# Pad rows, weight halves and weight loads in another order around the seam between routing and experts

## The chip, the cores and the metric

The kernel is one program on one core of a Trainium2 chip. The metric is the device time of one execution in microseconds (us). Of the kernel before there are three timed runs; the profiled execution is a fourth.

## The reference, cut to what matters

The layer is attention with a window of 64, followed by a mixture of experts: 2048 rows of 256 values, 16 experts of which each row goes to 4, and one shared expert that takes every row.

```python
h = _layernorm(x) * (1 + ca) + sa
x = x + ga * attention(h, w_qkv, w_out)          # 16 heads of 16, window 64
h = _layernorm(x) * (1 + cb) + sb
probs = softmax(abs((h @ ru.T) * silu(h @ rg.T)))
_, idx = top_k(probs + extra_bias, 4)            # 4 of 16 experts for a row
w = 1 + probs * extra_scale                      # taken at idx
y = sum over e of (silu(h @ Wg[e].T) * (h @ Wu[e].T)) @ Wd[e].T * c[:, e]
z = (silu(h @ Sg.T) * (h @ Su.T)) @ Sd.T
x = x + gb * (y + z)
```

Everything is float32. A product is made of three passes: each operand is split in a high half (rounded) and a low half (what the rounding left), and high by high, low by high and high by low are added.

## The kernel before, in words

**Stages.** `project_qkv` and `attention_and_routing` stand in one block of instructions, `experts_and_output` in a second. Between the two every engine reaches the end of its own list, drains, and waits until all have (the records of this are on L1999). The seam lies at about 312 to 338 us of the span.

**The end of the first block.** GpSimd sends the routed rows of the last tile pairs to `xs_scr` in DRAM by indirect DMAs (`dispatch`, `send_rows`, L140; one of 128 rows each). The rows of an expert are padded up to a multiple of 128: `fill_up` (L182 to L184) writes one block of 128 pad rows behind each of the 16 experts, as soon as the counts are known (`tb`). SyncE writes the pads of experts 0 to 10, ScalarE those of 11 to 15. An issue is a load of the place from `pad_i` and a DMA of 144 KB.

**Weights.** `raw` holds the 16 experts' weights: experts 0 to 7 are loaded in the attention stage, 8 to 14 by ScalarE at 290 us (semaphore `w_rest`), 15 by GpSimd in the second block (`w_last`, L190 and L191), which loads the shared expert's weights too (`sgu_raw`, `sdn_raw`). High halves are made by ScalarE: `split_hi` (L174 for gate and up, L175 for down). Low halves of gate and up are made by VectorE (`gu_low`, L1795, 128x704), those of down by GpSimd (`dn_low`, L1688, 88x512).

**The expert steps.** 79 steps of 128 rows of one expert each. For step s SyncE loads the rows (`load_x`, L1584, to `x_st`, four in flight: the first four at once, each further one after its buffer was transposed and `picked`), TensorE transposes them (L1859), ScalarE makes the high half of the transposed rows (L1620) and VectorE the low half (`x_lo`, L1743). TensorE makes gate and up (`GU`, L105), ScalarE the silu (L1626), VectorE the product (`gating`, L1755); that is transposed (`HT`, L1869), split (L1633, L1748) and multiplied by down (`YP`, L105). VectorE scales the result (L1763) and GpSimd sends it to `ys_scr` (L1709). The order of each engine's list is the order in the code. TensorE's list begins: transpose the rows of step 0, those of step 1, `GU` of step 0, transpose those of step 2, `GU` of step 1, transpose those of step 3, and so on. Step s of the first 16 waits for `gu_lo` of s + 1, and from step 2 on for `dn_lo` of s - 1.

**What sets the places of the halves.** `HI_IN_TAIL` is 11: `split_hi` of experts 0 to 10 stands in the first block. `LO_AHEAD` is 5: `gu_low` of five experts stands ahead of step 0, and `LOW_STEPS` lists the steps that each make one more. `FIRST` is 8.

Of the kernel before, what the change touches and what calls it, by code (L numbers as in the profile page):

```python
# [19 lines left out]
NE, TOPK, FI = 16, 4, 176  # L20
# [21 lines left out]
W_EXP = W_GU + W_DN  # L42
HW = D + 2 * NE
IDS = D + NE
HI_IN_TAIL, HI_AHEAD, LO_AHEAD = 11, 13, 5
LOW_STEPS = (0, 1, 3, 4, 5, 7, 8, 9, 11, 12, 13)
PLACES = TOPK * S_LEN
LD = 3 * 16

# [621 lines left out]
def attention_and_routing(nc, A, T, ctx, own):  # L671
# [122 lines left out]
    def _(eng):  # L794
# [78 lines left out]
        keep_x1(LAST, 3)  # L873
        keep_h2(PAIRS - 1, 1)
        eng.wait_ge(tb, TB_PAD)
        fill_up(nc, eng, A, T, 0, 11)
        for t in range(4):
            eng.wait_ge(x1_st[t], 32 * (TILES // 4) + 32)
            if t < 2:
# [4 lines left out]
    def _(eng):  # L884
# [102 lines left out]
        router_exp(PAIRS - 1, 1)  # L987
        for e in range(4, FIRST):
            split_hi(eng, T, e)
        eng.wait_ge(tb, TB_PAD)  # L990
        fill_up(nc, eng, A, T, 11, NE)
        eng.wait_ge(T["w_rest"], 64)
        for e in range(FIRST, HI_IN_TAIL):
            split_hi(eng, T, e)

    @block.gpsimd
# [460 lines left out]
def experts_and_output(nc, A, T, out, ctx, own):  # L1457
# [226 lines left out]
    @block.gpsimd  # L1684
    def _(eng):
        def dn_low(e):
            eng.wait_ge(w_hi2, 2 * e + 2)
            eng.tensor_tensor(lo[0:FH, e, W_GU:W_EXP], raw[0:FH, e, W_GU:W_EXP],  # L1688
                              dn_hi[0:FH, e, :].bitcast(F32), ALU.subtract).then_inc(dn_lo, 1)

        for e in range(3):
            dn_low(e)
        load_raw(eng, A, T, NE - 1, NE, w_last)
        eng.dma_start(sgu_raw[:, :, :, :], A["sgu"]).then_inc(sgu_ld, 16)
        eng.dma_start(sdn_raw[:, :, :], A["sd"]).then_inc(sdn_ld, 16)
        for e in range(3, FIRST):
            dn_low(e)
        for p in range(2):
            eng.wait_ge(sent[p], 32)

        def step(s, r, i, first, last):
            q = r // 2 % 2
            if r % 2 == 0 and runs(s, 4):

                eng.wait_ge(sent[q], 32 * i + 32)
                plain(eng)
            eng.wait_ge(y_out, s + 1)
            plain(eng)
            eng.indirect_dma_start(ys, bass.IndirectOffsetOnAxis(ap=ids_st[:, r:r + 1].bitcast(U32), axis=0), results(r % 8),  # L1709
                                   None).then_inc(sent[q], 16)  # L1710
            if isinstance(s, int) and FIRST + s < NE:
                dn_low(FIRST + s)

        for_steps(eng, step, NS)


        eng.wait_ge(y_mm, NS)
        for p in range(2):
            eng.wait_ge(sent[p], 32 + 16 * len([s for s in range(NS) if s // 2 % 2 == p]))
        for n, g in enumerate(LOADED):  # L1720
            load_planes(eng, g)
            if n % 2 == 0 and n < 6:
                load_add(eng, n // 2 + 1)


        k = 0
        for n in range(KEPT, TILES):
            if n % 2 == 0:
                eng.wait_ge(four_ld[n // 2], 16)
            if n % 4 == 0 or n == KEPT:  # L1730
                eng.wait_ge(add_ld[n // 4], 16)
            for a, b in ((planes[:, n, 0:2, :], planes[:, n, 2:4, :]), (planes[:, n, 0, :], planes[:, n, 1, :]),
                         (planes[:, n, 0, :], to_add[:, n, :])):
                if k % 3:
                    eng.wait_ge(fold, k)
                eng.tensor_tensor(a, a, b, ALU.add).then_inc(fold, 1)
                k += 1

    @block.vector
    def _(eng):  # L1740
# [54 lines left out]
            eng.tensor_tensor(lo[:, e, 0:W_GU], raw[:, e, 0:W_GU], gu_hi[:, e, :].bitcast(F32), ALU.subtract).then_inc(gu_lo, 1)  # L1795

        eng.memset(h_act[:, :, SH_I:SH_K * P], 0.0).then_inc(h_zero, 1)
        for e in range(3):
            gu_low(e)
        x_lo(0, 0)  # L1800
        x_lo(1, 1)
        for e in range(3, LO_AHEAD):
            gu_low(e)

        def step(s, r, i, first, last):
            p2 = r % 2
            gating(s, p2, GU[p2][:, FI:2 * FI], FI)
            x_lo(s + 2, p2)
            if runs(s, 2):
                y_gate(s - 2, (r - 2) % UNROLL, i if r % 4 >= 2 else i - 1)  # L1810
            if runs(s, 1):
                a_lo(s - 1, 1 - p2, FH, 2)
            if isinstance(s, int) and s in LOW_STEPS:
                gu_low(LO_AHEAD + LOW_STEPS.index(s))

            if isinstance(s, int) and s == NS - 4:
                eng.wait_ge(sdn_ld, 16)
                eng.tensor_tensor(sdn_raw[:, :, :], sdn_raw[:, :, :],
                                  gb[:, :].unsqueeze(1).broadcast_to([P, SH_K, D]), ALU.mult).then_inc(sdn_gb, 1)
            if isinstance(s, int) and NS - 3 <= s < NS - 1:  # L1820
                k = s - (NS - 3)
                eng.wait_ge(sh_hi, k + 1)
                eng.tensor_tensor(sgu_lo[:, k, :, :], sgu_raw[:, k, :, :], sgu_hi[:, k, :, :].bitcast(F32),
                                  ALU.subtract).then_inc(sh_lo, 1)
            if isinstance(s, int) and s == NS - 1:
                eng.wait_ge(sh_hi, 3)
                eng.tensor_tensor(sdn_lo[:, :, :], sdn_raw[:, :, :], sdn_hi[:, :, :].bitcast(F32), ALU.subtract).then_inc(sh_lo, 1)
# [264 lines left out]
```

## Time and profile before

| | us |
|---|---|
| median of 3 runs | 584.99 |
| lowest, highest | 582.08, 589.83 |
| profiled execution, its own time | 586.58 |
| span of its records | 584.8 |

1.8 us of the profiled execution lie outside its span. The granted clock over the span was 0.92 of full speed. Times in the rows count from the start of the span. "q" behind an engine's name means its sequencer, which issues DMAs, waits and drains; PEld is TensorE's weight load. DMA queue q0 is GpSimd's, q1 SyncE's, q10 ScalarE's.

### The profile page before, as it was taken

To read this page: it belongs to the slowest core of one execution; us is meant where nothing else is said; L and a number is where in the kernel's file an instruction comes from. 1 tells how busy PE (TensorE), PEld (TensorE's weight loads), DVE (VectorE), ACT (ScalarE), POOL (GpSimd) and SP (SyncE) were. 2 spreads that over 40 slices of the span, in tenths; PEclk is the share of its full clock that TensorE was granted. 3 is DMA by queue.
4 is the path that set the end of the run, shared out by engine and by line. 5 is a ranking of instruction groups with operands and counts; after the bars stand their busy time and mean duration, and the time that the engine had idled before them with its cause. 6 is when DMAs were issued, how large, how long until landed. Compare 5 with 4: busy or idle time off the path is not lost. (4 is left out here: it accounts for less than half of the span.)

```text
span 584.8 us, 12335 instructions
## 1 busy us (share of the span) xinstructions
PE 503.6 (86%) x3571; PEld 474.0 (81%) x3571; DVE 394.3 (67%) x1089; ACT 284.0 (49%) x743; POOL 288.3 (49%) x328
## 2 busy tenths in 40 slices
PE   2579899979999989999741088999999999999996
PEld 0379898979988989889641077899999999999996
DVE  2569954453677686876777299877776777775575
ACT  1447564434545445452244374555555555553331
POOL 0157820201044554654667599744444444446993
PEclk9788999996999999999755579999999999999998
DMA  6555797996574664823395553333434344446951
GB/s 153 150 159 167 203 271 189 286 226 162 132 192 131 178 173 121 225 81 91 87 343 180 178 191 103 109 126 125 134 123 131 124 129 128 131 148 236 415 203 72
DMA packets 62982, 98.00 MB, mean 168 GB/s; under 512 B 9747, under 2 KB 48210, under 8 KB 61574
## 3 DMA queue, kind: packets, MB, share of 16 engines
q1 hardware_dynamic: 50664, 57.80, 37.2%
q0 software_dynamic: 9136, 32.53, 14.6%
q10 hardware_dynamic: 3118, 6.89, 3.9%
q8 instruction: 31, 0.51, 0.4%
q14 instruction: 33, 0.27, 0.2%
HBM read 60.49 MB, written 40.04 MB: 172 GB/s over the span
## 5 line engine op out<-in xcount | busy, mean ns | idle before, releaser
L1709 POOL DMA_INDIRECT ys_scr<-h,ids_st x59 | 60.6, 1027 | 67.9 <-DVE h L1763 65.6
L140 POOL DMA_INDIRECT xs_scr<-h,slot_u x64 | 62.8, 980 | 54.9 <-PE TB L1312 26.7
L105 PE MATMUL GU<-gu_hi,xT 128*128 x316 | 84.4, 349 | 1.7 <-DVE xT L1743 1.7
L105 PE MATMUL YP<-dn_hi,aT 88*128 x316 | 67.2, 305 | 3.8 <-DVE aT L1748 3.8
L1633 ACT ACTIVATE aT<-HT 88x256 fp32r<-88x256 f32 (+1 forms) x95 | 37.8, 399 | 65.9 <-PE HT L1869 65.8
L1322 PE MATMUL O<-raw,prob 128*128 128x99 f32 x512 | 68.8, 282 | 0.0
L929 ACT ACTIVATE prob<-TB 128x512 f32<-128x512 f32 x64 | 38.2, 597 | 60.8 <-PE TB L1312 60.1
L1755 DVE TENSOR_TENSOR h_act<-GU,g_act 128x176 f32<-128x176 f32 (+1 forms) x95 | 35.2, 371 | 47.0 <-ACT g_act L1626 47.0
L1322 PEld LDWEIGHTS O<-raw,prob 128*128 128x128 f32 x512 | 64.2, 198 | 0.1
L105 PEld LDWEIGHTS YP<-dn_hi,aT 88*128 88x128 f32 x316 | 47.6, 188 | 10.6 <-issue 6.8
L105 PEld LDWEIGHTS GU<-gu_hi,xT 128*128 128x128 f32 x316 | 52.4, 193 | 2.2 <-issue 2.1
L1626 ACT ACTIVATE g_act<-GU 128x176 f32<-128x176 f32 (+1 forms) x95 | 32.4, 341 | 42.1 <-PE GU L105 42.0
L1748 DVE TENSOR_TENSOR aT<-HT,aT 88x256 fp32r<-88x256 f32 (+1 forms) x95 | 42.0, 442 | 15.6 <-ACT aT L1633 6.0
L105 PE MATMUL GU<-lo,xT 128*128 x158 | 51.8, 328 | 0.0
L1859 PE MATMUL XT<-ident,x_st 128*128 128x128 f32 x190 | 37.4, 279 | 15.7 <-DMA x_st<-xs_scr 15.5
L1054 DVE TENSOR_REDUCE neg_m<-SB 128x4 f32<-128x512 f32 x64 | 42.0, 686 | 9.4 <-PE SB L1300 9.0
L105 PE MATMUL YP<-lo,aT 88*128 x158 | 44.2, 280 | 0.0
L1859 PEld LDWEIGHTS XT<-ident,x_st 128*128 128x128 f32 x190 | 26.7, 144 | 19.2 <-DMA x_st<-xs_scr 16.4
L1743 DVE TENSOR_TENSOR xT<-XT,xT 128x256 fp32r<-128x256 f32 x95 | 39.9, 421 | 0.4 <-ACT xT L1620 0.3
L1312 PEld LDWEIGHTS TB<-gu_hi,dn_hi 97*128 97x128 f32 x240 | 37.6, 198 | 2.8
L1300 PEld LDWEIGHTS SB<-dn_hi,gu_hi 97*128 97x128 f32 x240 | 36.7, 193 | 2.7
L1869 PE MATMUL HT<-ident,h_act 128*88 128x128 f32 (+1 forms) x206 | 38.1, 273 | 0.0
(243 smaller groups left out, 1260.1 us busy)
## 6 DMA issues: line engine op xcount, KB each, us to landing
x_st<-xs_scr SPq DMA_DIRECT2D x79, 144.0 KB
dn_hi<-k_scr SPq DMA_DIRECT2D x48, 192.0 KB, 4.7
planes<-ys_scr POOLq DMA_DIRECT2D x8, 1024.0 KB, 17.1
k_scr<-raw SPq DMA_DIRECT2D x8, 768.0 KB, 6.4
dn_hi<-q_scr SPq DMA_DIRECT2D x24, 256.0 KB, 4.4
q_scr<-raw SPq DMA_DIRECT2D x8, 512.0 KB, 3.3
raw<-in_egu SPq DMA_DIRECT2D x8, 352.0 KB
raw<-in_x SPq DMA_DIRECT2D x16, 128.0 KB, 4.0
```

Of the source, the lines that this page charges most:

```text
L105: mm = eng.matmul(out, a, b, start=(i + j == 0), stop=(i == len(pairs) - 1 and j == 2))
L140: eng.indirect_dma_start(T["xs_scr"], bass.IndirectOffsetOnAxis(ap=T["slot_u"][:, par, t % 2, k:k + 1], axis=0), T["h2"][:, row, :], None) ...
L929: eng.activation(prob[:, q, :], TB[q % 2][:, :], ACT.Exp, scale=SCALE).then_inc(exp_done, 1)
L1054: eng.tensor_reduce(neg_m[:, p2, 4 * q:4 * q + 4], SB[q % 2][:, :].rearrange("p (h x) -> p h x", h=4), AX.X, ALU.max, negate=True).then_in ...
L1312: mm = eng.matmul(bank[:, hh * P:(hh + 1) * P], keys(par, 4 * q + hh, j), queries(n, t, 4 * q + hh), start=False, stop=True, skip_group_ch ...
L1322: mm = eng.matmul(O[:, head // 8, at:at + WIDE * VC], prob[:, q, hh * P:(hh + 1) * P], VW[:, bass.ds(HEADS * n + head, WIDE), :].rearrange ...
L1633: eng.activation(aT[0:rows, p2, 0, 0:k, :], HT[p2][0:rows, 0:k * P].rearrange("p (k x) -> p k x", k=k), ACT.Copy).then_inc(aT_hi, 1)
L1709: eng.indirect_dma_start(ys, bass.IndirectOffsetOnAxis(ap=ids_st[:, r:r + 1].bitcast(U32), axis=0), results(r % 8), None).then_inc(sent[q] ...
L1743: eng.tensor_tensor(xT[:, p2, 1, :, :], XT[p2][:, 0:D].rearrange("p (k x) -> p k x", k=KD), xT[:, p2, 0, :, :].bitcast(F32), ALU.subtract) ...
L1748: eng.tensor_tensor(aT[0:rows, p2, 1, 0:k, :], HT[p2][0:rows, 0:k * P].rearrange("p (k x) -> p k x", k=k), aT[0:rows, p2, 0, 0:k, :].bitca ...
L1859: mm = eng.transpose(XT[t % 2][:, k * P:(k + 1) * P], x_st[:, t, k * P:(k + 1) * P], ident[:, :])
L1869: mm = eng.transpose(HT[p2][0:rows, k * P:(k + 1) * P], h_act[:, p2, k * rows:(k + 1) * rows], ident[:, :])
```

## The change

Four edits. (1) SyncE writes the pads of experts 0 to 7 and ScalarE those of 8 to 15. (2) ScalarE waits for `w_rest` and makes the high halves of experts 8 and 9 ahead of its pads; expert 10 stays behind them. (3) VectorE makes two low halves of gate and up ahead of the rows' low halves instead of three, and four instead of five ahead of step 0; step 2 gets one, so that `LOW_STEPS` has 12 entries. (4) GpSimd issues its four loads ahead of all its low halves, and then waits until two low halves of gate and up are made; before, three of its own stood ahead of the loads.

```diff
+SP_PADS, HI_BEFORE_PADS = 8, 10
 HI_IN_TAIL, HI_AHEAD, LO_AHEAD = 11, 13, 5
-LOW_STEPS = (0, 1, 3, 4, 5, 7, 8, 9, 11, 12, 13)
+LOW_STEPS = (0, 1, 2, 3, 4, 5, 7, 8, 9, 11, 12, 13)
...
-        fill_up(nc, eng, A, T, 0, 11)
+        fill_up(nc, eng, A, T, 0, SP_PADS)
...
+        eng.wait_ge(T["w_rest"], 64)
+        for e in range(FIRST, HI_BEFORE_PADS):
+            split_hi(eng, T, e)
         eng.wait_ge(tb, TB_PAD)
-        fill_up(nc, eng, A, T, 11, NE)
-        eng.wait_ge(T["w_rest"], 64)
-        for e in range(FIRST, HI_IN_TAIL):
+        fill_up(nc, eng, A, T, SP_PADS, NE)
+        for e in range(HI_BEFORE_PADS, HI_IN_TAIL):
             split_hi(eng, T, e)
...
-        for e in range(3):
-            dn_low(e)
         load_raw(eng, A, T, NE - 1, NE, w_last)
         eng.dma_start(sgu_raw[:, :, :, :], A["sgu"]).then_inc(sgu_ld, 16)
         eng.dma_start(sdn_raw[:, :, :], A["sd"]).then_inc(sdn_ld, 16)
-        for e in range(3, FIRST):
+        eng.wait_ge(gu_lo, 2)
+        for e in range(FIRST):
             dn_low(e)
...
-        for e in range(3):
+        for e in range(2):
             gu_low(e)
         x_lo(0, 0)
         x_lo(1, 1)
-        for e in range(3, LO_AHEAD):
+        for e in range(2, LO_AHEAD - 1):
             gu_low(e)
...
-                gu_low(LO_AHEAD + LOW_STEPS.index(s))
+                gu_low(LO_AHEAD - 1 + LOW_STEPS.index(s))
```

GpSimd at the start of the second block, before (`raw`, `sgu_raw` and `sdn_raw` are the loads; `lo<-raw,dn_hi` is `dn_low`):

```order
L1688 TENSOR_TENSOR lo<-raw,dn_hi 88x512 x3
L190 DMA raw<-in_egu 128x704
L191 DMA raw<-in_ed 88x512
L1694 DMA sgu_raw<-in_sgu 128x1408
L1695 DMA sdn_raw<-in_sd 128x768
L1688 TENSOR_TENSOR lo<-raw,dn_hi 88x512 x5
L1709 DMA ys_scr<-y_st,ids_st 10752x256
```

and in the changed kernel, where the line numbers are higher by one to three:

```order
L191 DMA raw<-in_egu 128x704
L192 DMA raw<-in_ed 88x512
L1695 DMA sgu_raw<-in_sgu 128x1408
L1696 DMA sdn_raw<-in_sd 128x768
L1691 TENSOR_TENSOR lo<-raw,dn_hi 88x512 x8
L1711 DMA ys_scr<-y_st,ids_st 10752x256
```

Three subtractions moved from ahead of the four loads to behind them; all eight still stand ahead of the first result's DMA.

VectorE at the same place, before (`lo<-raw,gu_hi` is `gu_low`, `xT` the rows' low half, `h_act` the gating of a step):

```order
L1797 MEMSET h_act 128x2x32
L1795 TENSOR_TENSOR lo<-raw,gu_hi 128x704 x3
L1743 TENSOR_TENSOR xT<-XT,xT 128x256 x2
L1795 TENSOR_TENSOR lo<-raw,gu_hi 128x704 x2
L1755 TENSOR_TENSOR h_act<-GU,g_act 128x176
```

and in the changed kernel:

```order
L1799 MEMSET h_act 128x2x32
L1797 TENSOR_TENSOR lo<-raw,gu_hi 128x704 x2
L1745 TENSOR_TENSOR xT<-XT,xT 128x256 x2
L1797 TENSOR_TENSOR lo<-raw,gu_hi 128x704 x2
L1757 TENSOR_TENSOR h_act<-GU,g_act 128x176
```

The third low half moved behind the rows' low halves, and what was the fifth moved into step 0; step 2 takes the one that is then left over.

## Rows read from the trace of the kernel before

**Rows 1.** The page: the span of the records.

```profile
span 584.8 us, 12335 instructions
```

**Rows 2.** Stretches: length, busy us of PE, PEld, DVE, ACT, POOL, clock, DMA share, GB/s.

```profile
343.00:344.00 1.00, 1.00 (x6) 0.97 (x5) 1.00 (x2) 0.89 (x4) 1.00 (x2) 0.50 1.03 388
348.55:369.87 21.32, 18.16 (x124) 16.20 (x123) 20.51 (x38) 10.38 (x41) 19.93 (x16) 1.00 0.36 101
```

**Rows 3.** Line L1999, the seam: duration in ns, first and last start in us.

```profile
L1999 POOLq DRAIN  x1: 14062/14062/14062, 318.2 to 318.2; - x1
L1999 SPq DRAIN  x1: 7/7/7, 328.9 to 328.9; - x1
```

**Rows 4.** Line L184, the pads, the same columns.

```profile
L184 SPq DMA_DIRECT2D xs_scr<-in_pads x11: 517/517/639, 315.6 to 327.9; - x11
L184 ACTq DMA_DIRECT2D xs_scr<-in_pads x5: 524/535/635, 315.6 to 320.4; - x5
```

**Rows 5.** The timeline (start us, us, instruction, idle before) at the seam.

```profile
312.25 0.61 ACT L175 ACTIVATE dn_hi<-raw 88x512 fp32r<-88x512 f32 x1
325.34 0.96 POOL L140 DMA_INDIRECT xs_scr<-h,slot_u  x1 [0.30 <-issue]
```

**Rows 6.** DMA by queue: ScalarE's from 304 to 309.1, SyncE's from 326.5 to 330.5.

```profile
q10 hardware_dynamic: 331, 0.67, 39.4%
q1 hardware_dynamic: 107, 0.44, 38.3%
```

**Rows 7.** The timeline behind the seam, VectorE and ScalarE.

```profile
332.63 5.68 DVE L1795 TENSOR_TENSOR lo<-raw,gu_hi 128x704 fp32r<-128x704 f32 x3
338.24 0.74 DVE L1743 TENSOR_TENSOR xT<-XT,xT 128x256 fp32r<-128x256 f32 x2
342.00 0.33 DVE L1755 TENSOR_TENSOR h_act<-GU,g_act 128x176 f32<-128x176 f32 x1
348.55 0.34 DVE L1755 TENSOR_TENSOR h_act<-GU,g_act 128x176 f32<-128x176 f32 x1 [0.99 <-ACT g_act L1626]
337.12 0.38 ACT L1620 ACTIVATE xT<-XT 128x256 fp32r<-128x256 f32 x1 [0.71 <-PE XT L1859]
```

**Rows 8.** The same, TensorE.

```profile
336.40 0.69 PE L1859 MATMUL XT<-ident,x_st 128*128 128x128 f32 x2 [0.41 <-DMA x_st<-xs_scr]
338.80 0.95 PE L105 MATMUL GU<-gu_hi,xT 128*128 x2 [1.71 <-DVE xT L1743]
```

**Rows 9.** Line L1795: ns min/median/max, first and last start; four stretches.

```profile
L1795 DVE TENSOR_TENSOR lo<-raw,gu_hi x3: 1936/1949/1952, 332.6 to 336.4; 128x704 fp32r<-128x704 f32 x3
L1795 DVE TENSOR_TENSOR lo<-raw,gu_hi x4: 1070/1338/1957, 338.9 to 344.8; 128x704 fp32r<-128x704 f32 x4
L1795 DVE TENSOR_TENSOR lo<-raw,gu_hi x6: 1661/1692/1853, 349.9 to 367.0; 128x704 fp32r<-128x704 f32 x6
L1795 DVE TENSOR_TENSOR lo<-raw,gu_hi x3: 877/878/878, 372.3 to 376.9; 128x704 fp32r<-128x704 f32 x3
```

**Rows 10.** The timeline, GpSimd: the first and the last of its four loads.

```profile
337.52 0.62 POOL L190 DMA_DIRECT2D raw<-in_egu  x1
339.27 0.56 POOL L1695 DMA_DIRECT2D sdn_raw<-in_sd  x1
```

**Rows 11.** Line L1584, SyncE's issues of x_st: steps 0 and 1, 4, 5.

```profile
L1584 SPq DMA_DIRECT2D x_st<-xs_scr x2: 356/376/397, 333.1 to 334.0; - x2
L1584 SPq DMA_DIRECT2D x_st<-xs_scr x1: 333/333/333, 338.4 to 338.4; - x1
L1584 SPq DMA_DIRECT2D x_st<-xs_scr x1: 333/333/333, 339.3 to 339.3; - x1
```

**Rows 12.** SyncE's queue, packets, MB, share: 333.9 to 337.9; 340 to 341; 341 to 343.

```profile
q1 hardware_dynamic: 576, 0.59, 53.7%
q1 hardware_dynamic: 138, 0.14, 41.0%
q1 hardware_dynamic: 17, 0.02, 2.3%
```

## The prediction

> **What bounds the kernel now.** The page first: the span is 584.8 us [rows 1], and all four edits lie between 312 and 377 us of it, so the views are read there and not over the whole.
>
> At the seam I read the line of the drains. GpSimd's drain is posted at 318.2 and takes 14.06 us, so it ends at 332.3; SyncE reaches its own only at 328.9, and it takes 7 ns [rows 3]. So SyncE, which wrote the longer run of pads, is not what the seam waits for: it is 3.4 us ahead of GpSimd. GpSimd's last send of routed rows starts at 325.34 and takes 0.96 us, so it ends at 326.30 [rows 5]. What fills the 6.0 us from there to 332.3 no row names. It may be a time of its own, or GpSimd's rows may have to land first, or SyncE's pads disturb it.
>
> Behind the seam, VectorE is the first bound. Its three low halves of gate and up take 5.68 us from 332.63, then the low halves of the first two batches of rows (batch s is the 128 rows of step s) end at 338.98 (338.24 and 0.74), and only then TensorE can start `GU` of step 0, at 338.80, having waited 1.71 us for them [rows 7, 8]. Batch 1 had been transposed by 337.09 and had its high half at 337.50, so the rows were there before VectorE was. VectorE is still busy when step 0 wants its gating, at 342.00 [rows 7].
>
> From 348.55 to 369.87 VectorE is busy 20.51 of 21.32 us and GpSimd 19.93, while TensorE has 18.16 us of work [rows 2]. VectorE bounds this stretch, and it does because of the low halves: one takes 1.69 us while GpSimd makes its own or sends, 0.88 us once GpSimd has none left [rows 9]. Right behind the seam, beside GpSimd's subtractions without a pause, it takes 1.95 us.
>
> **Pads, edit 1.** SyncE's eleven issues start from 315.6 to 327.9, and ScalarE's five from 315.6 to 320.4 [rows 4]. From start to start that is 12.3 / 10 = 1.23 us and 4.8 / 4 = 1.20 us. Eight each end at 315.6 + 7 x 1.23 + 0.5 = 324.7 and 315.6 + 7 x 1.20 + 0.5 = 324.5. SyncE is done 3.7 us sooner. As GpSimd's drain ends 3.4 us behind SyncE already, this is worth nothing by itself. It is worth something only if the 6.0 us hang on data in flight: SyncE's queue still took 38.3% of the engines' time between 326.5 and 330.5 for 0.44 MB [rows 6], and that would now be gone. Bounds: +1 us (both queues at once slow GpSimd's rows while they overlap) and -3 us (the drain follows the last byte). I take -0.5 us, near nothing, because no row ties the drain to the pads.
>
> **High halves, edit 2.** Those of expert 7 end at 312.86 [rows 5]; two more experts at some 1.2 us each end at 315.3, before the first pad at 315.6. The wait for `w_rest` is over by then: ScalarE's queue moved its last 0.67 MB in the 5 us up to 309.1 [rows 6]. Expert 10 follows the pads, to 325.8, still 6.5 us ahead of GpSimd's drain. Nothing, either way.
>
> **Low halves, edits 3 and 4, with no change in the transfers.** GpSimd now issues its four loads first. They took from 337.52 to 339.83, 2.3 us [rows 10], so until 334.9 it subtracts nothing. VectorE's two low halves cost between 0.88 and 1.95 us each [rows 9]; I take 1.29, as one beside those loads took little more than the undisturbed one (it is between the two least of the second stretch, 1.07 and 1.34). They end at 335.2 instead of 336.4. VectorE then idles until batch 0 has its high half, at 336.4 (337.12 less the 0.71 that ScalarE idled), and again until batch 1 has its own, at 337.50 [rows 7]. `GU` of step 0 starts behind the transposes of batch 1, at 337.1: 1.7 us sooner than 338.80. But VectorE still has two low halves ahead of the first gating. They stand beside GpSimd's subtractions now, some 1.65 us each (between 1.34 and 1.95): from 337.9 to 341.2. The gating moves from 342.0 to 341.2, -0.8 us. Most of the head start ends in this queue.
>
> Then VectorE has twelve low halves in its steps instead of eleven. Step 2 takes the twelfth, where VectorE idled 0.99 us [rows 7]. It costs 1.07 to 1.69 us [rows 9], so 0.1 to 0.7 sticks out; I take +0.4. GpSimd's eight subtractions start at about 335 without a gap and end at 347 to 348.3, where they ended before; nothing waits for them sooner.
>
> **The loads and the rows on the same DMA engines.** This is what the edit moves that the diff doesn't say. SyncE issued the loads of batches 0 and 1 at 333.1 and 334.0 into an idle system: all four transfers, 576 packets, ran between 333.9 and 337.9 [rows 11, 12]. The loads of batches 4 and 5 were issued at 338.4 and 339.3, 0.8 and 1.8 us behind the first of GpSimd's loads [rows 10, 11]. Batch 4 got 138 packets through from 340 to 341, none sooner; then SyncE's queue passed 17 packets in 2 us [rows 12]. Now the first GpSimd load goes out at 332.6, and batches 0, 1, 2, 3 follow at +0.5, +1.4, +2.3, +3.1 us. Batches 0 and 1 should fare like batch 4: this moved 1.6 us after its issue instead of 0.9, so +0.7. Batches 2 and 3 should fare like batch 5: some 3 us late. For batch 1, +0.7 takes back 0.6 us of the gating's 0.8. Batch 2 is wanted by TensorE behind `GU` of step 0, at 340; 3 us late it holds it until 341, and `GU` of step 1 with it, where VectorE is the later one by little: +0.5 us. Bounds for the loads together: 0 (SyncE's packets pass unhindered) and +4 (batch 1 fares like batch 5).
>
> DMA: Bandwidth & Descriptors in the Trainium skill, Queues, rings and completion order, says that a DMA engine takes turns between its queues a packet at a time. By it the rows would only wait their turn and hardly be late; the two terms would be near 0. The trace does not bear this out fully: batch 4 passed like that, but 17 packets in 2 us is no fair turn.
>
> **The sum.** -0.5 (seam) - 0.8 (gating sooner) + 0.4 (step 2) + 0.6 + 0.5 (rows later) = +0.2 us. Behind 377 us nothing changes: every low half is made by then in both kernels. TensorE's clock is at 0.50 still in 343 to 344 [rows 2]; in this stretch VectorE sets the pace, so I count nothing for a rise that comes sooner. The profiled execution, 586.58 us, would become 586.8. It stands 1.6 us above the median of the three runs, so against those I forecast 585.2 us. That is no change. With the rows unhindered (the two last terms 0) the sum would be -0.9 and the time 584.1. A measurement of this kernel can tell about 2% (11.7 us) from none.
>
> **The rivals.**
>
> *Batch 1 shut out: slower, 588.* The mechanism: batch 1 fares like batch 5, since 1.4 us behind the first load is nearer to 1.8 than to 0.8. It arrives about 4 us late, at 340.4; `GU` of step 0, which stands behind its transpose, starts at 341.1 instead of 338.80, and the two low halves that now stand behind batch 1's push the first gating to 340.4 + 1.1 + 0.4 + 3.3 = 345.2, +3.2 us. It decides from the point where batch 1 lands after 338.2, for then the gating is later than 342.0. For it: the 17 packets. Against it: batch 4 passed beside the same loads. Sum: 585.0 - 0.5 + 3.2 + 0.4 = 588.1.
>
> *The drain follows the data: faster, 581.6.* Then -3 at the seam, and with the rows unhindered -0.8 + 0.4 behind it: 585.0 - 3.4 = 581.6. For it: SyncE's last pads were in flight until about 330, 2 us before the drain ended. Against it: GpSimd's drain need not know of another engine's transfers.
>
> *The batches take fair turns: 584.1.* Nothing behind the loads is late, and `GU` of step 0 starts at 337.1. Batch 4's 138 packets in 1 us speak for it, the 17 in 2 us against. This is what the page's rule gives.
>
> *VectorE and GpSimd fall in another phase: faster, 583.* Six low halves took 1.69 us where 0.88 is possible [rows 9]. If the shift of both lists lets them miss each other in part, up to 21.32 - 18.16 = 3.2 us can be won [rows 2]; two of it gives 583. It can as well go the other way by less than 1, as the low halves overlapped nearly throughout. Nothing in the rows picks a phase.
>
> **How the numbers follow.** Forecast 0.33, within 1.5 us of 585.2; fair turns 0.15; batch 1 shut out 0.22, drain 0.13, phase 0.12, and 0.05 for what I don't see. All cases lie within 1% of the time before, so within 2% gets 0.95; 0.02 and 0.03 remain for the sides, a little more for the slower one since the transfers have no bound from their own stretch. The three runs lie 582.08 to 589.83, so their median itself is uncertain by some 2 us. With the rivals' -3.4 and +3 the range is 581.0 to 589.2.
>
> **What would show it.** The line of the drains: SyncE's drain near 325.2, GpSimd's still ending at about 332; an end under 330.5 speaks for data in flight. Two low halves near 1 us each from 332.6, then VectorE idle, waiting for ScalarE's high half of the rows. TensorE's second transpose waiting for a DMA: until 337.1 is my case, past 338.5 the slower rival. First gating between 341 and 342.5. A low half in step 2 and gating of step 3 at about 348.7. The forecast is wrong if the step in which VectorE catches up is not there: if `GU` of step 0 is sooner by 1.7 us and step 4 still is.

## The result: 0.8 to 1.4% slower, and where the time went

| | before | changed |
|---|---|---|
| median of 22 runs, us | 587.38 | 590.74 |
| lowest, highest, us | 580.94, 609.77 | 585.39, 597.45 |
| profiled execution, its own time, us | 586.58 | 590.75 |
| span of its records, us | 584.8 | 588.9 |
| granted clock over the span | 0.92 | 0.913 |

The ratio of the runs is 1.0109 with a 95% interval of 1.008 to 1.0138, so by it the change costs some 6.4 us (0.0109 x 587.38), at least 4.7 (0.8% of 587.38). The ratio is of the fast runs of both kernels; the medians of all 22 lie 3.4 us apart. Forecast were no change and 585.2 us, with a range of 581.0 to 589.2.

Single runs of one kernel lie 12 us apart and more (before, 580.94 to 609.77). In the profiled executions most of such a spread arises ahead of the seam: e15 and e16 left out, GpSimd's last send of routed rows ends anywhere from 319.6 to 334.5 us, although the kernels hardly differ up to there. So I measure times from the end of GpSimd's drain (D) on. Kernels with the same code behind the seam then agree within 0.3 us to the gating of step 40 and within 0.8 us to the end.

**The three stretches.** The stage table from D to the first gating, on to the gating of step 40, and on to the end (columns: stretch, its length, busy us of each engine, granted clock, DMA share, GB/s); first of the kernel before, whose D is at 332.26, then of the changed one, whose D is at 332.53.

```profile
332.26:342.00 9.74, 4.58 (x15) 3.73 (x16) 9.39 (x9) 6.10 (x15) 9.44 (x9) 0.50 0.54 156
342.00:435.24 93.24, 89.41 (x627) 83.87 (x627) 73.45 (x169) 54.36 (x204) 56.65 (x50) 0.99 0.41 126
435.24:584.80 149.56, 144.57 (x1042) 139.59 (x1040) 99.05 (x231) 70.75 (x240) 82.66 (x89) 0.98 0.49 170
```

```profile
332.53:347.00 14.47, 6.34 (x20) 4.67 (x20) 9.76 (x8) 7.98 (x19) 12.15 (x12) 0.50 0.57 186
347.00:440.30 93.30, 90.09 (x621) 84.67 (x622) 73.20 (x170) 52.59 (x199) 51.15 (x46) 0.97 0.37 114
440.30:588.90 148.60, 143.27 (x1042) 138.59 (x1040) 98.94 (x231) 70.61 (x240) 82.88 (x89) 1.00 0.49 171
```

D itself is 0.27 us later. The first stretch is 4.7 us longer (14.47 against 9.74), the second is the same. The third is 1.0 us shorter, with the same work in it and a clock of 1.00 against 0.98. So the whole loss lies in the first 15 us behind the seam.

**The seam.** The line of the drains in the changed kernel (ns, then the start), answering to [rows 3]:

```profile
L2001 POOLq DRAIN  x1: 14757/14757/14757, 317.8 to 317.8; - x1
L2001 SPq DRAIN  x1: 7/7/7, 324.9 to 324.9; - x1
```

SyncE reaches its drain 4.0 us sooner, as the edit meant, and GpSimd's still ends last, at 317.77 + 14.76 = 332.53.

**Behind the seam.** The changed kernel's timeline, VectorE, then GpSimd, then TensorE (start, us, engine, line, what; in brackets the idle time before and what ended it), answering to [rows 7, 8]:

```profile
332.90 1.65 DVE L1797 TENSOR_TENSOR lo<-raw,gu_hi 128x704 fp32r<-128x704 f32 x2
337.24 0.42 DVE L1745 TENSOR_TENSOR xT<-XT,xT 128x256 fp32r<-128x256 f32 x1 [2.69 <-ACT xT L1623]
339.35 0.42 DVE L1745 TENSOR_TENSOR xT<-XT,xT 128x256 fp32r<-128x256 f32 x1 [1.68 <-ACT xT L1623]
339.69 7.31 DVE L1797 TENSOR_TENSOR lo<-raw,gu_hi 128x704 fp32r<-128x704 f32 x2
346.92 0.33 DVE L1757 TENSOR_TENSOR h_act<-GU,g_act 128x176 f32<-128x176 f32 x1
```

```profile
335.03 0.55 POOL L1696 DMA_DIRECT2D sdn_raw<-in_sd  x1
335.59 9.86 POOL L1691 TENSOR_TENSOR lo<-raw,dn_hi 88x512 fp32r<-88x512 f32 x8
```

```profile
338.20 0.69 PE L1861 MATMUL XT<-ident,x_st 128*128 128x128 f32 x2 [1.42 <-DMA x_st<-xs_scr]
338.86 0.95 PE L106 MATMUL GU<-gu_hi,xT 128*128 x2
341.71 0.69 PE L1861 MATMUL XT<-ident,x_st 128*128 128x128 f32 x2 [0.73 <-DMA x_st<-xs_scr]
347.31 0.65 PE L1871 MATMUL HT<-ident,h_act 128*88 128x128 f32 x2 [2.72 <-DVE h_act L1757]
```

Two low halves take 7.31 us. The line's own durations over that stretch (min/median/max, ns) split them:

```profile
L1797 DVE TENSOR_TENSOR lo<-raw,gu_hi x2: 878/3694/6511, 339.7 to 346.1; 128x704 fp32r<-128x704 f32 x2
```

The third low half was asked for at 339.69, 0.4 us into the fourth of GpSimd's eight subtractions, and took 6.51 us: until 346.2, when the run was over (335.59 + 9.86 = 345.45) and 0.75 us more had passed, about the 0.88 that the fourth then took alone. GpSimd's eight went through at 9.86 / 8 = 1.23 us as if nobody else were there. `GU` of step 0 started at D + 6.33 (before: D + 6.53), but its gating stood behind those two low halves in VectorE's list, and TensorE idled 2.72 us for it. In the kernel before, VectorE took 1.95 us beside GpSimd's first run [rows 9].

### The profile page after: what moved, and what is told of

It reads as the page before. It is cut to its first block and busy times, and to the rows that moved or that the text cites. A ratio compares the mean times of both kernels' runs of the same rounds, so it can differ in the third digit from the quotient of the medians.

```text
span 588.9 us, 12336 instructions
## 1 busy us (share of the span) xinstructions
PE 507.1 (86%) x3571; PEld 476.6 (81%) x3571; DVE 393.0 (67%) x1089; ACT 284.0 (48%) x743; POOL 285.2 (48%) x328
## 5 line engine op out<-in xcount | busy, mean ns | idle before, releaser
L1325 PE MATMUL O<-raw,prob 128*128 128x99 f32 x512 | 71.4, 289 | 0.0
L1325 PEld LDWEIGHTS O<-raw,prob 128*128 128x128 f32 x512 | 66.7, 205 | 0.0
L1303 PEld LDWEIGHTS SB<-dn_hi,gu_hi 97*128 97x128 f32 x240 | 38.2, 201 | 2.9
```

The source lines that it names most:

```text
L1303: mm = eng.matmul(bank[:, hh * P:(hh + 1) * P], queries(n, t, 4 * q + hh), keys(par, 4 * q + hh, j), start=False, stop=True, skip_group_ch ...
L1325: mm = eng.matmul(O[:, head // 8, at:at + WIDE * VC], prob[:, q, hh * P:(hh + 1) * P], VW[:, bass.ds(HEADS * n + head, WIDE), :].rearrange ...
```

## The experiments

All kernels compute the full result. "Shut out" is short for a low half of gate and up that takes until GpSimd's run of subtractions ends. The table has the later reading of all of them (e15 and e16 ran on a slower chip, see there); times are us, from D, and the ratio is to the kernel before on the same chip (with its interval where it was timed). "third" is the low half that comes right behind those made alone.

| kernel | third: asked at, took | first gating | step 40 | end | ratio |
|---|---|---|---|---|---|
| before | | 9.73 | 102.98 | 252.5 | 1 |
| changed | 7.16, **6.51** | 14.40 | 107.74 | 256.4 | 1.0109 (1.0080 to 1.0138) |
| e1 seam only | | 9.74 | 102.88 | 251.9 | 0.9984 (0.9921 to 1.0047) |
| e2 halves only | 7.45, **6.23** | 14.40 | 107.57 | 255.9 | 1.0044 (0.9997 to 1.0091) |
| e3 gaps | 7.05, 0.88 | 9.73 | 103.80 | 252.4 | 0.9991 (0.9944 to 1.0037) |
| e4 wait for four | 7.26, 0.88 | 9.43 | 103.95 | 252.9 | 1.0040 (1.0002 to 1.0077) |
| e5 restart | 6.94, 1.73 | 10.47 | 104.09 | 253.1 | one run |
| e6 late loads | 5.53, 1.41 | 7.69 | 102.17 | 251.0 | 0.9989 (0.9943 to 1.0035) |
| e7 drain wait | | 9.73 | 102.83 | 251.7 | 1.0083 (1.0045 to 1.0122) |
| e8 four alone | 5.62, 2.67 | 8.22 | 102.48 | 251.3 | 0.9962 (0.9907 to 1.0016) |
| e9 pause behind 1st | 6.99, 1.95 | 10.74 | 103.61 | 252.7 | one run |
| e10 pause behind 2nd | 6.92, 0.88 | 9.60 | 104.30 | 253.0 | one run |
| e11 late loads, no pauses | 5.51, 1.06 | 8.37 | 101.94 | 250.7 | 1.0055 (1.0005 to 1.0104) |
| e12 three alone | 5.64, 0.88 | 8.33 | 101.39 | 250.0 | 1.0029 (0.9981 to 1.0077) |
| e13 fourth from a pause | 8.23, 1.94 | 11.98 | 104.36 | 252.9 | one run |
| e14 third, unbroken | 5.60, **8.03** | 16.61 | 109.85 | 258.6 | one run |
| e15 wait ahead of the run | 13.37, 1.17 | 16.34 | 112.27 | 261.8 | one run |
| e16 loads last | 8.88, 1.11 | 11.79 | 111.19 | 260.0 | one run |
| e17 seventh, no loads | 9.57, 1.94 | 13.30 | 106.56 | 255.5 | one run |
| e18 second, unbroken | 4.37, **9.24** | 16.59 | 109.91 | 258.6 | one run |

The ratios of the experiments rest on 6 to 12 runs each and tell 1% at best. e11 shows it: its ratio says slower (1.0005 to 1.0104), while from D it is 1.0 us ahead of the kernel before at step 40. What the experiments show, they show in the columns from D.

**Which edits (e1, e2).** e1 is the kernel before with edits 1 and 2, e2 with edits 3 and 4.

> The kernel before with the edits at the seam alone (pads 8 and 8, high halves of experts 8 and 9 ahead of ScalarE's pads). Theory A (the loss of some 4 us arises behind the seam, where one low half of VectorE took 6.5 us in the changed kernel): time within 0.3% of the kernel before; GpSimd's drain ends about 6 to 6.6 us behind its last send, as in both kernels; longest low half on VectorE under 2 us. Rival B (the two pad queues at once lengthen the drain, and the loss is there): slower by 0.5% or more.

> The kernel before with the edits behind the seam alone (order of low halves, GpSimd's loads first, its wait for two low halves). Theory A: the whole loss, 0.7 to 1.2%; one low half of VectorE stretched to 5 us or more, first gating 4 to 5 us later after the seam than before (14.4 us behind the end of the drain instead of 9.7). Rival B: no slower than the kernel before by 0.3%.

e1's drains:

```profile
L2002 POOLq DRAIN  x1: 14101/14101/14101, 311.4 to 311.4; - x1
L2002 SPq DRAIN  x1: 7/7/7, 318.6 to 318.6; - x1
```

SyncE is done 6.9 us ahead of the end of GpSimd's drain (311.4 + 14.1), before 3.4 us, and GpSimd's drain still ends 5.96 us behind its last send. All of e1's columns are those of before, and all of e2's those of the changed kernel, within 0.7 us. The loss belongs to edits 3 and 4: theory A in both.

**Is it the unbroken run (e3, e4)?** In e3 each of GpSimd's seven further subtractions waits for the one ahead of it: no work more or less, only a wait between.

```diff
+            if 0 < e < FIRST:
+                eng.wait_ge(dn_lo, e)
```

> The changed kernel, but each of GpSimd's subtractions of experts 1 to 7 waits for the one before it to be counted, so that its run of eight has a pause behind each. Theory A with a run without pauses as the cause: VectorE's low halves beside them fall to 2 us or less each, first gating about 9.5 to 10 us behind the drain instead of 14.4, time 3 to 4 us less than the changed kernel, about that of the kernel before. Rival C (the loss comes from batches 1 and 2 that land late beside GpSimd's loads): the low half is shorter, but the time stays within 1 us of the changed kernel's. Rival A2 (VectorE is shut out whatever pauses there are): one low half still over 5 us.

e3's timeline, VectorE and GpSimd, then TensorE at batch 2 (D is 325.89):

```profile
332.95 2.75 DVE L1799 TENSOR_TENSOR lo<-raw,gu_hi 128x704 fp32r<-128x704 f32 x2
335.62 0.33 DVE L1759 TENSOR_TENSOR h_act<-GU,g_act 128x176 f32<-128x176 f32 x1
328.96 13.29 POOL L1693 TENSOR_TENSOR lo<-raw,dn_hi 88x512 fp32r<-88x512 f32 x8
...
335.43 0.69 PE L1863 MATMUL XT<-ident,x_st 128*128 128x128 f32 x2 [1.19 <-DMA x_st<-xs_scr]
```

Two low halves take 2.75 us (0.88 and 1.95) instead of 7.31, the first gating is at D + 9.73 instead of 14.40, and GpSimd pays with 13.29 us for its eight, which nothing waits for. 3.9 of the 4.8 us at step 40 are back. Theory A stands; rivals C and A2 are out. This is the clearest run of the study: the loss is VectorE being shut out, not the sum of the low halves.

e4 lets GpSimd begin only when VectorE's four are done.

```diff
-        eng.wait_ge(gu_lo, 2)
+        eng.wait_ge(gu_lo, 4)
```

> The changed kernel, but GpSimd waits for four low halves of gate and up instead of two before its eight subtractions. Theory A: the two low halves behind the batches take 0.9 us each, first gating about 9.5 us behind the drain (batch 1 lands late, at 338.2 after a drain at 332.5, then 0.7 + 0.4 + 1.8 us), but the run of eight starts at about 341.6 and shuts out the low half of step 0 until 351, so the time is no better than the changed kernel's by more than 1 us, and step 2 waits for dn_lo. Rival A3 (VectorE was shut out only because it asked in the middle of a run that had begun; a run that begins while VectorE is at work takes turns, as in the kernel before): low halves near 1.9 us and the time 3 us less.

```profile
343.48 1.68 DVE L1797 TENSOR_TENSOR lo<-raw,gu_hi 128x704 fp32r<-128x704 f32 x2
346.95 1.56 DVE L1797 TENSOR_TENSOR lo<-raw,gu_hi 128x704 fp32r<-128x704 f32 x1
345.25 6.34 POOL L1691 TENSOR_TENSOR lo<-raw,dn_hi 88x512 fp32r<-88x512 f32 x4 [5.99 <-DVE lo L1797]
```

The third and fourth are made alone, 1.68 us for both. The next, at 346.95, falls into the second subtraction of a run without a wait in it, and is served in 1.56 us. An unbroken run is thus not enough, and the low half of step 0, which theory A had shut out, is not; step 40 is 3.8 us sooner than in the changed kernel, as rival A3 had it. But here a wait of 5.99 us lies between GpSimd's DMA issues and its run.

**Loads and drain (e5 to e8).** e5 cuts the run once, behind the second subtraction, by a wait for batch 1's high half (`xT_hi2`, 2). e6 is e3 with the four loads moved behind the third subtraction. e7 is the kernel before, with a wait of GpSimd at the end of its first list for its rows to have landed. e8 is the kernel before with four low halves ahead of the rows' instead of three; GpSimd waits for them (`gu_lo`, 4), then issues its loads, then makes all eight subtractions with e3's waits.

> The changed kernel, but GpSimd's run of eight subtractions is cut once: after two it waits until batch 1 has its high half (about 6.7 us behind the drain), then runs the other six without a pause. VectorE's third low half then asks in the first subtraction of a new run, instead of in the fourth of one run. Theory P (what shuts VectorE out is that it asks late in a run; it asked in the first or second one in the kernel before and in the run that waited for four, and got its turn): third low half 1.3 to 2.0 us, first gating about 9.5 to 10 us behind the drain, and 252 to 253 us from the drain's end to the end of the span instead of 256.4. Theory K (any run without pauses shuts VectorE out when it comes from other work): third low half over 5 us again, first gating at 14 us or later.

> The changed kernel with the pauses in GpSimd's run, and with its four loads behind its third subtraction instead of ahead of the first, so that the first four batches have the DMA engines alone. Theory D (the loads made batches 1 and 2 late by 1.4 and 4.2 us, and that is the last 0.8 us that the kernel with pauses stands behind the kernel before at step 40): batches 0 to 3 land at 3.0, 4.1, 4.9, 5.6 us behind the drain, first GU at 4.8 to 5, first gating at 8 to 8.7, step 40's gating at 102.3 to 103.0 instead of 103.8. Rival: step 40 stays at 103.8, since VectorE's low halves bound the steps anyway.

> The kernel before, with one addition: at the end of its first list GpSimd waits until all its routed rows have landed. In six traces the drain ended 3.0 to 3.2 us behind the landing of the last row, and never less than 5.96 us behind the end of the last send. Theory L (the drain takes 3 us from the landing, whatever is done): end of drain at the landing + 3.0 to 3.2, nothing gained. Theory F (the drain has a fixed length from the last send, 5.96 us, and the landing only by chance before it): same end. Rival W (the drain's own poll is what takes long, and a list that has waited drains at once, as SyncE's does in 7 ns): drain ends within 1 us of the landing, 2 us gained.

> A version that should beat both. From the kernel before: VectorE makes four low halves ahead of the rows' low halves and one behind them; GpSimd waits for these four, then issues its loads, then its eight subtractions with a pause behind each. Low halves one to four stand alone: 0.85 to 0.88 us each, done 3.8 us behind the drain. The loads go out from 3.9 on, when batches 0 to 3 are all issued or on their way: these land as in the kernel before. First GU at 4.9 instead of 6.5, first gating at 7.7 to 8.3 instead of 9.7; the low halves in the steps stay below 2.0 us each. Step 40's gating at 101.5 to 102.5 instead of 103.0: 0.5 to 1.5 us faster than the kernel before (0.1 to 0.25%), 4 to 5.5 us faster than the changed kernel. Rival: GpSimd's run ends 2 us later than before, so that VectorE's low halves are disturbed for longer, and step 40 is no sooner than 103.0.

e5: one cut is enough (1.73 us, not 6.5). e6, TensorE's second and third transpose (D is 328.56):

```profile
332.61 0.69 PE L1865 MATMUL XT<-ident,x_st 128*128 128x128 f32 x2 [0.26 <-DMA x_st<-xs_scr]
333.37 0.95 PE L106 MATMUL GU<-gu_hi,xT 128*128 x2
335.29 0.63 PE L1865 MATMUL XT<-ident,x_st 128*128 128x128 f32 x2
```

With no loads beside them batches 0 to 3 land at D + 3.06, 4.00, 4.93 and 5.61, in the changed kernel at D + 3.52, 5.63, 9.14 and 10.32. TensorE no longer waits for batch 2, and `GU` of step 0 starts at D + 4.81. Against e3, e6 gains 2.0 us at the first gating and 1.6 at step 40. That puts the price of the loads beside the rows at 1.6 us; e11, the same without the waits in the run, stands at 101.94, which puts it at up to 1.9. Both also start GpSimd's subtractions sooner than e3, so this is not the loads' price alone.

e7, GpSimd's drain:

```profile
L2001 POOLq DRAIN  x1: 5955/5955/5955, 335.7 to 335.7; - x1
```

This answers what fills the 6.0 us that no row named. The list waits until the last row has landed (335.46), and then the drain takes 5.96 us once more, so that it ends 3 us later than it would without the wait; theories L and F had it end at the same time, W sooner. In all 19 other traces D is the later of two, to 0.02 us: 5.96 us behind GpSimd's last send, or 3.0 behind the landing of its last rows (changed kernel: 6.63 and 3.00; before: 5.96 and 3.19). SyncE's pads appear in neither. e8's four low halves take 3.26 us together, but its fifth, asked for while GpSimd was still issuing loads, 2.67: it ended 0.75 us behind the first subtraction.

**What in the run decides it (e9, e10, e13, e14).** e9 and e10 keep one wait of e3's seven, behind the first or the second subtraction. Both serve the third low half, asked for in the third from the pause (e9) or just as the second begins (e10; there it went first, in 0.88 us, and the subtraction took 2.00, so e10 says less). Two readings were left: that the place counted from the last wait decides (up to the third served, the fourth not), or that DMA issues directly ahead of the run do, with no wait between. e13 has e9's pause and lets VectorE wait until four subtractions are made (`dn_lo`, 4), so that it asks in the fourth from the pause; e14 has no pause and moves the third low half ahead of the rows' own, behind a wait for two (`dn_lo`, 2), so that it is asked for in the third of the run.

> The changed kernel with one pause in GpSimd's run, behind its first subtraction. VectorE's third low half asks some 7.0 to 7.3 us behind the drain, in the fourth subtraction; counted from the pause this is the third of the run. Theory P (how far into an unbroken run VectorE asks decides; asked in the first or second it gets the next turn, in the fourth it waits until the run is over): either a low half of 2 us or less and first gating at 9.5 to 10.5 us (then the threshold is between third and fourth), or one over 5 us and gating at 14 us or later (then between second and third). Rival Q (any pause in the run heals, wherever it is): 2 us or less. Rival R (a pause heals only if it falls in VectorE's wait): over 5 us.

> The changed kernel with one pause, behind GpSimd's second subtraction: VectorE asks in the second subtraction from the pause. Theory P: low half of 2 us or less, first gating 9.5 to 10.5 us behind the drain, the drain's end to the end of the span 252 to 253.5 us. Rival R (a pause heals only if it falls in VectorE's wait): over 5 us, gating at 14 us or later, 256 us.

> The changed kernel with a pause behind GpSimd's first subtraction, and VectorE waits for four subtractions before its third low half. It then asks in GpSimd's fifth subtraction, the fourth from the pause, at about 8.3 us behind the drain. Theory P (asked in the fourth or later of an unbroken run, it waits until the run is over): low half of 4.5 to 5.5 us, done at 13 to 13.8; first gating 14 us or later. Rival Q (any pause in the run heals): low half under 2.1 us, first gating 11.5 to 12.5.

> The changed kernel without any pause, but VectorE's third low half stands ahead of the rows' low halves and waits for two subtractions of GpSimd, so it asks in the third of the unbroken run of eight, at about 5.6 us. Theory P with its threshold between the third and the fourth: low half of 2.0 us or less, and the run then takes turns with VectorE's next low half. Rival Q (only a pause, or an ask in the first two, is served): low half over 6 us, done when GpSimd's run ends at about 12.9 us.

VectorE in e13, then VectorE and GpSimd in e14:

```profile
345.14 3.82 DVE L1799 TENSOR_TENSOR lo<-raw,gu_hi 128x704 fp32r<-128x704 f32 x2 [1.07 <-POOL lo L1693]
```

```profile
337.57 8.03 DVE L1797 TENSOR_TENSOR lo<-raw,gu_hi 128x704 fp32r<-128x704 f32 x1 [3.57 <-POOL lo L1691]
...
335.04 9.80 POOL L1691 TENSOR_TENSOR lo<-raw,dn_hi 88x512 fp32r<-88x512 f32 x8
```

Fourth from a pause: served, 1.94 us (3.82 with the next). Third of the unbroken run: shut out for 8.03 us. Both ran on one chip. The place counted from the last subtraction's pause is refuted.

**From the other side (e15, e16).** e16 moves the loads behind the eight subtractions and leaves the run unbroken. e15 puts a wait between the loads and the run. Both ran on a chip on which the kernel before took 613.69 us; their D is at 352.29 and 354.03, some 20 us later than in the two kernels above.

> The changed kernel, but GpSimd waits for batch 0's high half between its loads and its eight subtractions; these then run from about 4.4 us behind the drain without a pause, and VectorE's third low half asks at about 7.0, in the third. Theory L (what shuts VectorE out is a run that follows GpSimd's DMA issues without a break): low half of 2.0 us or less, first gating 9.5 to 11 us. Theory N (a run of all eight without a pause, wherever it starts, shuts out who asks from the third on): low half over 6 us, done when the run ends at about 14.3; first gating 15.5 us or later.

> The changed kernel with GpSimd's four loads behind its eight subtractions. The run starts at about 2.0 us behind the drain with no DMA issue ahead of it, and VectorE's third low half asks at about 5.5, in the third. Theory L: low half of 2.0 us or less. Theory N: low half over 5 us, done when the run ends at about 12. Step 2 waits for the last expert's weights in either case, so the times behind it say nothing.

e16, VectorE and GpSimd:

```profile
362.91 2.98 DVE L1797 TENSOR_TENSOR lo<-raw,gu_hi 128x704 fp32r<-128x704 f32 x2
358.32 12.50 POOL L1691 TENSOR_TENSOR lo<-raw,dn_hi 88x512 fp32r<-88x512 f32 x8 [10.26 <-DVE lo L1797]
```

The third low half is asked for 4.6 us into an unbroken run of eight, in its fourth, where the changed kernel's was, and is served in 1.11 us. e15 tells nothing: its rows came so late (first gating at D + 16.34) that the low half met only the first subtraction, which began 7.3 us behind the last load.

One count was still left. e16's run began behind a real wait for the two low halves (10.26 us of idle time, the seam's drain included), so its fourth subtraction is also the fourth instruction since GpSimd last waited; in the changed kernel the four issues make it the eighth, in e14 the seventh. e17 is e16 with VectorE waiting until six subtractions are made (`dn_lo`, 6): the seventh since the wait, no issues. e18 is e14 with a wait for one (`dn_lo`, 1): the sixth, with issues.

> The kernel with GpSimd's loads behind its eight subtractions, in which VectorE's third low half also waits until six of GpSimd's are made, so that it is asked for in the seventh instruction since GpSimd last waited, with no DMA issue among the seven. If issues directly ahead of the run shut VectorE out, it is served here: 0.9 to 2.0 us. If it is the count of instructions since GpSimd's last wait, issues counted too (it was 7 and 8 where VectorE was shut out, 4 at most where an unopposed run began behind a wait and it was served), it waits for the rest of the run, through the seventh and eighth, and takes 2.9 to 3.4 us.

> The changed kernel with the third low half ahead of the rows' own, asked for when one of GpSimd's subtractions is made, so in the second of the unbroken run behind the four loads: the sixth instruction since its last wait. If issues directly ahead of the run decide alone, it is shut out from there to the run's end: 9.0 to 9.5 us, and the first gating comes some 1 us later than with the ask in the third (16.6 behind the drain). If it is a count since the last wait with a threshold of seven, it is served in under 2 us, and the first gating comes at 10 to 12 behind the drain.

VectorE and GpSimd in e17, then in e18:

```profile
345.48 3.80 DVE L1797 TENSOR_TENSOR lo<-raw,gu_hi 128x704 fp32r<-128x704 f32 x2 [3.88 <-POOL lo L1691]
338.01 10.52 POOL L1691 TENSOR_TENSOR lo<-raw,dn_hi 88x512 fp32r<-88x512 f32 x8 [8.07 <-DVE lo L1797]
```

```profile
336.88 9.24 DVE L1797 TENSOR_TENSOR lo<-raw,gu_hi 128x704 fp32r<-128x704 f32 x1 [2.35 <-POOL lo L1691]
335.57 9.80 POOL L1691 TENSOR_TENSOR lo<-raw,dn_hi 88x512 fp32r<-88x512 f32 x8
```

Both came out for the issues, again on one chip. e17's seventh is served in 1.94 us. e18's sixth is shut out for 9.24 us, until 0.75 us behind the run's end at 345.37, as the changed kernel's was (346.20 and 345.45). e18's first gating, expected 1 us later than e14's, came at the same time, D + 16.59. What sets the duration is only when VectorE asks: the later, the shorter.

**Versions that might beat both (e11, e12).** e11 is e6 without the waits in the run. e12 is the kernel before with three low halves of VectorE's made alone, two of GpSimd's behind them, then the loads, then six with waits:

```diff
-        for e in range(3):
+        eng.wait_ge(gu_lo, 3)
+        for e in range(2):
             dn_low(e)
...
-        for e in range(3, FIRST):
+        for e in range(2, FIRST):
```

> The changed kernel with GpSimd's four loads behind its third subtraction, and without pauses. VectorE asks at about 5.5 us, in or behind the third subtraction of a run of three, which the loads then end. Theory P or R alike: shut out for no longer than the run's rest, low half 1.4 us; the second run, of five, begins at about 8 us, when VectorE's low half of step 0 asks in its first: first gating at 7.7, step 40 at 102.2 to 103 as with pauses. Rival: the second run shuts out the low half of step 0 or 1 for up to 6 us; step 40 at 104 or later.

> A candidate in which GpSimd alone is changed against the kernel before: it waits for the three low halves ahead of the rows' low halves, makes two subtractions, issues its loads, makes the other six, with a pause behind each. Low halves one to three at 0.87 us each, done 2.8 us behind the drain; loads from 5.6 us on, batches 0 to 3 on time; first GU at 4.85, first gating at 7.7 to 8.7; step 40's gating at 101.7 to 102.5 against 102.9, so 0.4 to 1.2 us faster than the kernel before. Rival: the eight subtractions end later than 16 us behind the drain and disturb one more low half in the steps: step 40 at 102.9 or later.

e12's stages from its D, as above:

```profile
331.50:339.83 8.33, 4.86 (x16) 4.03 (x17) 5.94 (x9) 6.06 (x16) 5.27 (x7) 0.50 0.44 106
339.83:432.89 93.06, 89.37 (x626) 83.20 (x625) 73.39 (x170) 54.06 (x203) 59.96 (x52) 0.99 0.43 134
432.89:581.45 148.56, 143.61 (x1042) 138.60 (x1040) 98.35 (x231) 70.75 (x240) 82.77 (x89) 1.00 0.49 171
```

It reaches the gating of step 40 1.6 us sooner than the kernel before, the best of all. The ratio, 0.9981 to 1.0077, does not confirm that: it excludes a gain of over 0.2%, though 1.6 us is 0.3%. Since the first part of the program strews by several us, I don't claim a faster kernel.

## Why the prediction was wrong, step by step

**The baseline.** Of the 5.5 us between 585.2 and 590.74, 2.4 belong to the kernel before, whose median is 587.38 over 22 runs and not 584.99 as over three. The rest is the change.

**The seam, -0.5.** Measured +0.27; from the last send to D it is 6.63 us instead of 5.96, since the last rows landed 3.6 us behind that send instead of 2.8. SyncE's drain came at 324.87, forecast 325.2. That the drain doesn't follow SyncE's pads is shown by e1 (5.96 us again), and that waiting for the landing gains nothing by e7. The rival "the drain follows the data", which meant SyncE's pads, is out; GpSimd's own rows can hold the drain, as they did here. High halves, edit 2: nothing, as forecast; e1 covers both.

**Two low halves from 332.9.** Forecast 1.29 us each, measured 0.85 and 0.88, with VectorE idle behind them as forecast.

**Low halves behind the batches: the step that failed.** The text put the two "beside GpSimd's subtractions now, some 1.65 us each (between 1.34 and 1.95): from 337.9 to 341.2", -0.8 us. They began at 339.69 and took 7.31 us together (6.51 and 0.88) instead of 3.3, and the first gating came 4.67 us later behind D than before, not 0.8 sooner. The rival on the phase looked at the right place and bounded it wrongly ("the other way by less than 1"). The price was read from rows in which both engines take turns [rows 9]. What it missed is how edit 4 lets GpSimd's run begin: directly behind four DMA issues, and with VectorE idle. Before, VectorE was within a low half when a run began, or started one within 0.1 us:

```profile
332.56 5.01 POOL L1688 TENSOR_TENSOR lo<-raw,dn_hi 88x512 fp32r<-88x512 f32 x3 [6.26 <-POOLq L1999]
338.91 3.17 DVE L1795 TENSOR_TENSOR lo<-raw,gu_hi 128x704 fp32r<-128x704 f32 x2
339.83 8.43 POOL L1688 TENSOR_TENSOR lo<-raw,dn_hi 88x512 fp32r<-88x512 f32 x5
```

The range had an end for the loads (+4) and none for this. The cause is shown by removal (e3, e5, e9, e10), by taking the loads from ahead of the run (e16, e17), and by making it worse (e14, e18).

SBUF — State Buffer in the Trainium skill, Who interferes with whom, says that a VectorE instruction with two inputs in SBUF contends with a GpSimd instruction that reads there, and that the port pair they share is an exclusive lock for which the order of issue decides who blocks. The trace agrees as to who is hit: the low halves of rows, whose one input is TensorE's product, took 0.42 us at 339.35 inside GpSimd's run, and 0.42 at 350.83 with GpSimd idle. As to how long, a lock held for one instruction would give a wait of the rest of the one subtraction under way, 1.26 us at most (an estimate, with the duration from the traces). The served low halves agree: in e5, e9, e13, e16 and e17 the third ended 0.75 us behind the one subtraction that it was asked for in. The changed kernel does not: there the wait lasted through five.

**Rows beside the loads, +0.6 and +0.5.** The direction was right, the size too small. Batch 0 was 0.5 us late (forecast 0.7), batch 1 1.5 (0.7), batch 2 4.2 (some 3). `GU` of step 0 started at 338.86, forecast 337.7. By e3 against e6 the two terms are worth up to 1.6 at step 40, not 1.1. "Fair turns" is out. "Batch 1 shut out" has the nearest time, 588.1, and was not what happened: batch 1 landed at 338.16, just short of its own point of 338.2, and `GU` of step 0 was not late at all.

**Step 2's extra low half, +0.4.** It took 0.88 us at 352.88, under the forecast's 1.07, GpSimd making no subtraction then. The low halves of steps 0 and 1 took 0.88 and 0.87 for the same reason, before 1.39 and 1.07, and so steps 0 to 2 regained 0.7 us (the lag behind the kernel before, measured from D, is 4.67 us at step 0's gating and 3.93 at step 2's). Step 3 gave it back (5.47). There TensorE worked without a gap and at half clock, 0.50 until 353.5 (1.2 GHz), where before it had 1.00 (2.4 GHz) from 344.1 on. So "I count nothing for a rise that comes sooner" did not hold for one that comes later.

**What would show it.** The text gave 341 to 342.5 for the first gating. The 346.92 of the changed kernel told at first sight which step had failed, and the line of the low halves by how much.

**What stays open.** Why a run behind DMA issues isn't broken into: no row looks inside. Being directly behind issues is also not the whole condition. In the kernel before and in e11 a run follows issues as directly, but VectorE is within a low half when it begins, and they share it. The loads' own traffic is not the cause: in e9 and e13 the same loads are in flight, and VectorE is served. And every run without issues ahead begins behind a wait, so that issues and a missing wait are told apart by the count of instructions alone (e17 against e18). The ratio says 6.4 us, the medians of all runs 3.4, and the traces 4.8 at step 40 and 3.9 at the end, from D. The traces lie about at or under the lower end of the ratio's interval (4.7), and nothing in them accounts for more.

## What to carry to other kernels

Ask of every instruction that is moved what it stands directly behind, on both engines that share something: a price read where two engines alternate holds only for that order. If GpSimd's arithmetic has to follow its own DMA issues, put something it really waits for between, and check in the trace how long VectorE's first overlapping instruction takes. Where runs strew in one part and the change lies in another, measure from an event between them.

## What the runs showed of the hardware

- A VectorE subtraction of 128x704 with both inputs in SBUF takes 0.85 to 0.88 us alone, 1.9 to 2.0 in turns with GpSimd's, and 6.2 to 9.2 when it comes into an unbroken run of GpSimd's right behind DMA issues (shut out: the changed kernel, e2, e14, e18; not over 2.0: e3, e5, e9, e10, e13, e16 and e17, with a wait in the run or no issues ahead of it). Shut out, it ends 0.75 us behind the run; served, 0.75 us behind the subtraction that it was asked for in (e5, e9, e13, e16, e17).
- A low half asked for during GpSimd's DMA issues took between 0.88 us (e12, and the changed kernel's second) and 2.67 (e8); 1.29 in the kernel before, 1.96 in e11.
- GpSimd's drain ended at the later of 5.96 us behind its last send and 3.0 us behind the landing of its last rows, in 19 traces. With a wait for the landing ahead of it (e7), it took 5.96 us from there.
- Loads of 1.6 MB from GpSimd's queue, issued ahead of 144 KB batches on SyncE's, made the third of these land 4.2 us later (D + 9.14 in the changed kernel, D + 4.90 in the kernel before).
